# A fused four-layer block on one core: the first group's scores in halves of the ring's rows, ScalarE normalising the second batch, the Hadamard products moved behind the group

## What is computed

```python
# x: (4, 512, 256) fp32; HIDDEN 256, 16 heads of 16
def attn_a(x, Wq, bq, Wk, bk, Wv, bv, Wo, bo):
    Q, K, V = (split_heads(x @ W.T + b) for W, b in ((Wq, bq), (Wk, bk), (Wv, bv)))   # (B, 16, 512, 16)
    attn = softmax(Q @ K^T / sqrt(16), axis=-1)
    return merge_heads(attn @ V) @ Wo.T + bo
def ffn(x, W1, W2, W3):                      # H = 1024
    hidden = silu(x @ W1.T) * (x @ W3.T)
    return fwht(hidden) @ W2.T               # Walsh-Hadamard transform, normalised
def attn_b(x, Wv, Wg, bg, Wq, bq, Wo):
    store = (x @ Wv) * sigmoid(x @ Wg + bg) * sqrt(0.05)
    mem = scan(store, decay=0.95, axis=1)
    return (mem * sigmoid(x @ Wq + bq) * sqrt(0.05)) @ Wo
x = x + attn_a(layernorm(x)); x = x + ffn(layernorm(x))
x = x + attn_b(layernorm(x)); x = x + ffn(layernorm(x))
```

## Time and profile before

| what | us |
|---|---|
| median of 3 runs (586.34 to 586.47) | 586.35 |
| the profiled execution's own time | 586.26 |
| its span, first to last instruction | 584.4 |
| PE busy | 565.8 (97%) |
| DVE busy | 376.8 (64%) |
| ACT busy | 298.5 (51%) |
| POOL busy | 176.6 (30%) |

### The profile page before, as it was taken

How to read it: one execution, slowest core, us unless ns; L and a number is a source line. 1 busy time by engine, 2 the same in 40 slices (tenths; PEclk the granted TensorE clock), 3 DMA queues, 4 the chain that set the end, 5 groups by cost and what they waited for, 6 DMA issues and landing times.

```text
span 584.4 us, 8867 instructions
## 1 busy us (share of the span) xinstructions
PE 565.8 (97%) x3288; PEld 390.1 (67%) x3288; DVE 376.8 (64%) x718; ACT 298.5 (51%) x546; POOL 176.6 (30%) x193
## 2 busy tenths in 40 slices
PE   9899999999999988999999999999999999999997
PEld 4534334344334433368888888898777888888886
DVE  5498898898888899644363444558887436344433
ACT  3238878876886787752334242244445233424221
POOL 3956446354455242820101010014333010101000
PEclk9999999999999999999999999999999999999999
DMA  7654740240033030010000000000000010010101
GB/s 231 135 112 163 199 122 18 76 127 20 2 111 109 3 146 3 3 72 2 1 0 1 1 0 1 2 2 0 1 0 2 1 36 1 1 36 2 38 0 37
DMA packets 17891, 26.54 MB, mean 45 GB/s; under 512 B 2552, under 2 KB 10744, under 8 KB 17464
## 3 DMA queue, kind: packets, MB, share of 16 engines
q1 hardware_dynamic: 15992, 24.13, 13.6%
q10 hardware_dynamic: 1856, 1.84, 1.4%
HBM read 10.88 MB, written 5.24 MB: 28 GB/s over the span
## 4 chain that ended last, share of the span: by engine, by line
PE 85%; DVE 5%; ACT 4%; issue 2%; DMA 1%; POOL 1%; SPq 1%; DVEq 0%; ACTq 0%
PE PS L281 82%; PE PS L292 2%; DVE mxr L861 2%; ACT PR L735 1%; DMA ring<-ql 1%; DVE PR L1020 1%; ACT xf L644 1%; ACT qf L658 1%; DVE XNs L842 1%; ACT PR L788 1%; POOL xTl L1051 1%; ACT xTh L644 1%; PE PS L472 1%; DVE AOl L853 1%; SPq L214 1%
## 5 line engine op out<-in xcount | busy, mean ns | idle before, releaser
L281 PE MATMUL PS<-xTh,ring 128*128 128x512 f32 x608 | 188.5, 392 | 0.0
L861 DVE TENSOR_REDUCE mxr<-PS 128x1 f32<-128x512 f32 x256 | 163.0, 682 | 29.0 <-PE PS L281 28.7
L735 ACT ACTIVATE PR<-PS 128x512 f32<-128x512 f32 x256 | 137.8, 603 | 39.7 <-PE PS L281 39.7
L281 PEld LDWEIGHTS PS<-xTh,ring 128*128 128x128 f32 x608 | 113.2, 188 | 22.9 <-issue 0.8
L281 PE MATMUL PS<-xTl,ring 128*128 128x512 f32 x304 | 110.3, 391 | 0.4 <-POOL xTl L1051 0.4
L281 PE MATMUL PS<-ring 50*128 50x512 f32 (+1 forms) x512 | 98.2, 450 | 5.4 <-DVE mxr L861 4.9
L975 DVE TENSOR_TENSOR PR<-PR,PS 128x512 f32<-128x512 f32 x64 | 43.8, 684 | 91.6 <-PE PS L281 73.7
L281 PEld LDWEIGHTS PS<-ring 50*128 50x128 f32 (+1 forms) x512 | 41.2, 184 | 84.2 <-ACT PR L735 57.2
L644 ACT ACTIVATE AOh<-PR 128x512 fp32r<-128x512 f32 x72 | 45.5, 632 | 101.1 <-DVE PR L975 89.2
L1051 POOL TENSOR_TENSOR xTl<-xf,xTh 128x512 fp32r<-128x512 f32 x30 | 43.2, 1456 | 140.9 <-ACT xTh L644 140.9
L853 DVE TENSOR_TENSOR AOl<-PR,AOh 128x512 fp32r<-128x512 f32 x72 | 51.1, 710 | 50.3 <-ACT AOh L644 50.3
(11 more groups left out here) (98 smaller groups left out, 621.5 us busy)
## 6 DMA issues: line engine op xcount, KB each, us to landing
ring<-qh SPq DMA_DIRECT2D x52, 128.0 KB, 3.1
ring<-ql SPq DMA_DIRECT2D x26, 128.0 KB, 3.1
ring<-weight_scratch SPq DMA_DIRECT2D x3, 1024.0 KB, 4.9
weight_scratch<-in_w SPq DMA_DIRECT2D x2, 1024.0 KB, 6.8
out<-X SPq DMA_DIRECT2D x8, 256.0 KB, 2.2
X<-in_x SPq DMA_DIRECT2D x3, 512.0 KB, 5.2
PR<-in_w SPq DMA_DIRECT2D x1, 1024.0 KB, 7.6
ring<-AOh SPq DMA_DIRECT2D x8, 128.0 KB, 4.0
```

The costliest lines, as they stand in the source:

```text
L281: return nc.tensor.matmul(dst, lhsT, rhs, start=start, stop=stop, skip_group_check=True)
L735: nc.scalar.activation(PR[:, j % 8, :], PS[:, kq_bank(j), :], ACT.Exp, scale=HD ** -0.5)\
L861: nc.vector.tensor_reduce(mxr[:, S % 2, blk, TT * p + t:TT * p + t + 1], PS[:, QK0 + i % 3, :], AX.X, ALU.max, negate=True).then_inc(max_d ...
```

## The change

It does six things.

1. The twelve row copies for n = 0 and 1 are all issued by SP, first the six of row block 1, then the six of row block 0, each half with its own semaphore (`first_rows[blk]`). ACT issues none, and SP no longer waits for the first twelve before it issues those for n = 2 and 3.
2. The first sixteen score tiles are taken as eight of row block 1, then eight of row block 0 (`first_score`); from tile 16 on in pairs as before.
3. `keep_busy` ahead of the transposes goes from 7 to 4, the one ahead of the projections from 512 to 384 columns, and of the five between values and scores one is left. In units 9, 10 and 12 no fill is left.
4. The Hadamard products stand behind units 8, 9, 10 and 12. ACT's copies of them come after `mT`, and the split of batch 1's first transposed tile comes before the fourth one's.
5. ACT normalises batch 1 in two steps per tile (subtract the mean, multiply by the deviation's reciprocal), from a negated mean that POOL writes (`nmean`). POOL's own normalising (L1054) goes, and POOL splits the group's maxima ahead of `place_values`.
6. The eight DMAs of `wo` are issued by SP behind `max_rows(0)`; `WOh` is written by ACT in step K = 3 and `WOl` by POOL in step K = 5.

```diff
-HAD_AT = (4, 5, 6, 8)
+HAD_AT = (8, 9, 10, 12)
...
+        nmean = sb("nmean", [P, TT])
...
+        first_rows = [sem(f"first_rows{blk}") for blk in range(2)]
...
+        def first_score(i):
+
+            return (i % 8, i // 8) if i < 16 else (i // 2, i % 2)
...
-            ring_load(0, 0)
-
-            for n in range(2):
-                sp.wait_ge(ring_in[n], QDMAS)
+
+            for blk in (1, 0):
+                for n in range(2):
+                    copies = ring_rows(0, n, 0)[2 * blk:2 * blk + 2]
+                    sp.wait_ge(qk_hi, n + 1)
+                    for args in copies:
+                        sp.dma_start(*args).then_inc(first_rows[blk], DMA)
+                    copies = ring_rows(0, n, 1)[blk:blk + 1]
+                    sp.wait_ge(qk_lo, n + 1)
+                    for args in copies:
+                        sp.dma_start(*args).then_inc(first_rows[blk], DMA)
             ring_load(0, 2)
             ring_load(0, 3)
             max_rows(0)
+
+            for e in range(2):
+                for j in range(GH):
+                    r = 32 * j + HD * e
+                    sp.dma_start(OT[r:r + HD, :, :].rearrange("p a c -> p (a c)").rearrange("p (g n) -> p g n", n=D),
+                                 wo.rearrange("(g e) (j c) n -> e j c g n", e=2, c=32)[e, j, 0:HD, :, :])\
+                        .then_inc(wo_in, DMA)
...
-            def score_qk(U, h):
+            def score_qk(U, h, n=None):
                 b, p, t = U // STEPS, U % STEPS // TT, U % TT
-                i, blk = 2 * U + h, 1 - h
+                i, blk = 2 * U + h if n is None else n, 1 - h
...
-                    pe.wait_ge(ring_in[2 * mt], QDMAS * (b + 1))
-                    pe.wait_ge(ring_in[2 * mt + 1], QDMAS * (b + 1))
+
+                    pe.wait_ge(ring_in[2 * mt], QDMAS * (b + mt))
+                    pe.wait_ge(ring_in[2 * mt + 1], QDMAS * (b + mt))
...
+                if 2 * K + h < 3:
+
+                    pe.wait_ge(w2h_done, 2 * K + h + 1)
...
+                if a == 0:
+                    pe.wait_ge(w2h_done, FT // 2)
...
-            keep_busy(7, MB, SEQ)
+            keep_busy(4, MB, SEQ)
...
-            keep_busy(1, MB, SEQ)
+            keep_busy(1, MB, FILL)
...
-            keep_busy(2, PS[:, 5, :], SEQ)
-            pe.wait_ge(ring_in[0], QDMAS)
-            keep_busy(3, PS[:, 5, :], SEQ)
+            keep_busy(1, PS[:, 5, :], SEQ)
             pe.wait_ge(qk_hi, 4)
             pe.wait_ge(qk_lo, 4)
-            for U in range(LEAD):
-                for h in range(2):
-                    wait_qk(U, h)
-                    score_qk(U, h)
-                if U == 4:
-
-                    pe.wait_ge(fly_done, 3)
-                    pe.wait_ge(v_copied, 2)
-                if U in HAD_AT:
-                    j = HAD_AT.index(U)
-                    mm(PS[:, HAD_BANK[j], :], had[:, :], PR[:, 4 + j, :], True, True).then_inc(had_ready, 1)
-                elif U < 8:
+            for i in range(2 * LEAD):
+                U, h = first_score(i)
+                if i in (0, 8):
+                    pe.wait_ge(first_rows[1 - h], QDMAS)
+                if i >= 3:
+                    pe.wait_ge(max_done, i - 2)
+                score_qk(U, h, i)
+                if i % 2 and U < 8:
                     keep_busy(1, MB, FILL)
-                elif U == LEAD - 2:
-                    pe.wait_ge(xns_ready, 1)
-                    pe.wait_ge(mt_ready, 1)
-                    ln_transpose(0, MB)
-                else:
-                    pe.wait_ge(w2h_done, 3)
-                    keep_busy(1, PS[:, 2, :], FILL)
-                if U == 8:
-                    pe.wait_ge(ml_done, 1)
-                    nc.tensor.transpose(MB[0:32, 0:P], ms[:, :, :, :].rearrange("p a b k -> p (a b k)"), ident[:, :])\
-                        .then_inc(mps_ready, 1)
-            pe.wait_ge(w2h_done, FT // 2)
+                elif i % 2:
+
+                    if U == 8:
+                        pe.wait_ge(fly_done, 3)
+                        pe.wait_ge(v_copied, 2)
+                    if U in HAD_AT:
+                        j = HAD_AT.index(U)
+                        mm(PS[:, HAD_BANK[j], :], had[:, :], PR[:, 4 + j, :], True, True).then_inc(had_ready, 1)
+                    if U == 8:
+                        pe.wait_ge(ml_done, 1)
+                        nc.tensor.transpose(MB[0:32, 0:P], ms[:, :, :, :].rearrange("p a b k -> p (a b k)"), ident[:, :])\
+                            .then_inc(mps_ready, 1)
+                    if U == LEAD - 2:
+                        pe.wait_ge(xns_ready, 1)
+                        pe.wait_ge(mt_ready, 1)
+                        ln_transpose(0, MB)
...
-                act.wait_ge(ring_in[(n + 2) % 4], QDMAS * (b + (n > 1)))
+                act.wait_ge(ring_in[(n + 2) % 4], QDMAS * b)
...
-                if n == 1:
-                    for part, ready in ((0, qk_hi), (1, qk_lo)):
-                        act.wait_ge(ready, 2)
-                        for args in ring_rows(0, 1, part):
-                            act.dma_start(*args).then_inc(ring_in[1], DMA)
             for half in range(2):
                 v_evacuate(0, half, PS[:, V_BANK[half], :])
-            for n in range(2):
-                act.wait_ge(ring_in[n], QDMAS)
-
-            for e in range(2):
-                for j in range(GH):
-                    r = 32 * j + HD * e
-                    act.dma_start(OT[r:r + HD, :, :].rearrange("p a c -> p (a c)").rearrange("p (g n) -> p g n", n=D),
-                                  wo.rearrange("(g e) (j c) n -> e j c g n", e=2, c=32)[e, j, 0:HD, :, :])\
-                        .then_inc(wo_in, DMA)
+
+            act.wait_ge(nmean_done, 1)
+            act.wait_ge(rstd_done, 2)
+            act.wait_ge(lnT_ready, 2)
+            for t in range(TT):
+                nc.scalar.activation(XNs[:, t, :], X[:, TT + t, :], ACT.Identity, bias=nmean[:, t:t + 1])\
+                    .then_inc(centred, 1)
+            for t in range(TT):
+                c = slice(TT + t, TT + t + 1)
+                act.wait_ge(centred, t + 1)
+                last = nc.scalar.activation(XNs[:, t, :], XNs[:, t, :], ACT.Copy, scale=rstd[:, c])
+            last.then_inc(xns_ready, 1)
             for j in range(FT // 2):
+                if j == 0:
+                    max_evacuate(0)
                 if j == FT // 2 - 1:
-                    max_evacuate(0)
+                    ln_evacuate(1, 0, MB)
+                    ln_hi(1, 0, 0)
                 act.wait_ge(had_ready, j + 1)
                 hi(hadamard_part(j), PS[:, HAD_BANK[j], :], 1.0 / HID ** 0.5)
                 hi(W2h[:, 2 * j:2 * j + 2, :].rearrange("p f n -> p (f n)"), PS[:, HAD_BANK[j], :], 1.0 / HID ** 0.5)\
                     .then_inc(w2h_done, 1)
-            act.wait_ge(wo_in, 8 * DMA)
-            hi(WOh[:, :, :].rearrange("p g n -> p (g n)"), OT[:, :, :].rearrange("p a c -> p (a c)")).then_inc(whi_done, 1)
-            ln_evacuate(1, 0, MB)
...
+                if K == 3:
+                    act.wait_ge(wo_in, 8 * DMA)
+                    hi(WOh[:, :, :].rearrange("p g n -> p (g n)"), OT[:, :, :].rearrange("p a c -> p (a c)"))\
+                        .then_inc(whi_done, 1)
...
-            for U in range(LEAD):
-                for h in range(2):
-                    row_max(U, h)
+            for i in range(2 * LEAD):
+                row_max(*first_score(i), i)
...
+                    pool.wait_ge(mom_done, 2)
+                    nc.gpsimd.tensor_scalar(nmean[:, :], mom[:, TT:2 * TT, 0], -1.0, None, ALU.mult).then_inc(nmean_done, 1)
...
+            split_max(0)
             for g in range(GROUPS):
                 place_values(0, g)
-
-            pool.wait_ge(rstd_done, 2)
-            pool.wait_ge(lnT_ready, 2)
-            for t in range(TT):
-                last = normalise_tile(TT + t, TT + t, t)
-            last.then_inc(xns_ready, 1)
-            split_max(0)
-            pool.wait_ge(whi_done, 4)
-            lo(WOl[:, :, :].rearrange("p g n -> p (g n)"), OT[:, :, :].rearrange("p a c -> p (a c)"),
-               WOh[:, :, :].rearrange("p g n -> p (g n)")).then_inc(wol_done, 1)
...
+                if K == 5:
+                    pool.wait_ge(whi_done, 4)
+                    lo(WOl[:, :, :].rearrange("p g n -> p (g n)"), OT[:, :, :].rearrange("p a c -> p (a c)"),
+                       WOh[:, :, :].rearrange("p g n -> p (g n)")).then_inc(wol_done, 1)
```

8 lines of the change are left out of this document (4 added, 4 removed).

## The result

The changed kernel takes 594.85 us in the median of four executions (593.57 to 598.37); the kernel before, run four times beside it, 586.35 (585.37 to 586.47). The ratio is 1.0158, 95% interval 1.0114 to 1.0203: slower by 1.6%, where 579.6 was forecast. The profiled execution took 594.78.

A forecast was written before the change was run, and what follows sets the result against it. The prediction took PE to be 85% of the chain, with gains only where PE is not the limit. From 586.26, -7.3 to the first score tile and +0.55 to the first exponential gave 579.5, stated as 579.6; range 578.6 to 582.3.

The forecast's parts named there:

- Row copies, the landing: Ahead of the scores: the sixth row copy, issued by SP at 16.1, lands 3.8 us later, at 19.9.
- The rival of the late landing: Ahead of the scores: the sixth copy takes 6.2 us to land although SP is alone, total 582.0; chance 0.08.
- a landing grows with what is queued ahead and not behind: Row copies: argument that the second six do not delay the first; otherwise 583.4 instead of 579.6.
- T0: Start of the first score tile's matmul: forecast 19.95 against 27.25 before, a gain of 7.3 us.
- DVE's 0.64 still sets the pace: Score stage: tiles taken by row block load as many columns, so DVE's maxima stay 0.64 us apart.
- the rival "falls once": PE gaps near 7.5, 9.8 and 19.8: one 5.15 us slow stretch costs 2.6, total 582.2; chance 0.05.
- the rival "slower": Less fill in units 9 to 12 lowers PE's clock, which stays low in the loop over K; 589.6; chance 0.03.
- The shift of the start: Ahead of the transposes: fewer fills move all projections 2.05 us earlier, bounds 1.7 and 2.3.
- The cost of the moved Hadamard products: Maxima to exponentials: ACT's four Hadamard pairs put the first exponential 0.55 us later behind T0, bounds -0.1 and +1.5.
- Tile 8 did not wait for its rows: Score stage: the twelfth copy, needed at 25.1, causes no wait; the worst landing costs 1.0 us.
- ACT's normalising: Ahead of the scores' end: eight half-size ACT instructions, 23.2 to 28.0, cost nothing; without cover up to 4.8 us.
- The rule on partition halves that the prediction weighed: Row copies: halves serialize, read as none landing before the whole; the rival had total 583.4, chance 0.03.

The follow-up runs named there:

- a_pairs_fill9: The changed kernel with its first sixteen tiles in pairs of both row blocks, waiting for all twelve copies, and nine fills ahead instead of one; 587.01 us.
- a_ones_late: The changed kernel with the four ones-rows DMAs issued behind all the row copies instead of ahead of them; 581.74 us.
- a_fill4: The changed kernel with four fills instead of one ahead of the first score tile; median 584.43 us, ratio 0.9970 to the kernel before.
- a_ones_fill2_s256: a_ones_late with two fills ahead of the first tile and 256 columns in the fills between pairs; median 580.10 us, ratio 0.9898 to the kernel before.
- a_gate: The changed kernel with SP waiting until the first six row copies have landed before it issues the other six; 593.88 us.
- a_pairs: The changed kernel with its first sixteen tiles in pairs of both row blocks, as before, so waiting for all twelve copies; 589.50 us.
- b_nofill: The kernel before with one fill instead of five between values and scores; 585.98 us.
- b_start4_early: The kernel before with the changed kernel's shorter fills at the start, and its five later fills all ahead of the wait for rows; median 587.59 us, ratio 1.0013.
- a_s512: The changed kernel with 512 instead of 384 columns in the first group's eight fills between pairs; 599.49 us.
- a_fill5_s256: The changed kernel with five fills ahead of the first tile and 256 columns in the fills between pairs; median 583.14 us, ratio 0.9949 to the kernel before.

## Why the prediction was wrong

**What failed, in the order of the steps.**

- *Row copies, the landing.* The step took 3.8, the landing of two copies "behind four of its own, in a quiet stretch"; it measured 6.1. The rival of the late landing had the right size (6.2) for a wrong reason, the input loads. Shown: the four ones-rows DMAs, moved away, give 4.0. They were in the trace ahead of the copies, and the step gave them no effect on the landing. The argument that a landing grows with what is queued ahead and not behind missed too: with the ones-rows in place it was 4.9 with the next six copies held back, 6.1 with them following. T0 was 22.90 instead of 19.95; of the 2.95, 22.90 - 20.49 = 2.41 went with these DMAs (2.1 in the landing, 0.35 in SP's issue, which took 1.34 for the first two copies instead of 1.82). The other 0.54 is 0.24 of issue (16.34 against 16.1), 0.2 of landing and 0.1 until PE starts.
- *"Both halves' matmuls load as many columns, so DVE's 0.64 still sets the pace."* The columns are the same, but two neighbours of different row blocks take 0.43 until the next load (a_pairs_fill9) and two of one row block 0.62 to 0.66 (a_ones_late, a_fill4). With the fill of 384 columns a pair takes 1.50, and DVE waits 0.21 for each. From T0 to the first exponential this costs 20.37 - 18.70 = 1.67 (a_ones_late against a_ones_fill2_s256). The Trainium skill, page "TensorE: Matmul & The Clock Gate", section "Why this matters for your kernels", says that matmuls of few rows in distinct row groups run concurrently; the 0.43 against 0.66 agrees, and the rule spoke against this order.
- *The clock.* This is the step that decided. The forecast took a clock that stays up; the rival "falls once" priced a fall at 2.6, half of the start's slow 5.15 us; the rival "slower" had the mechanism, PE at its lower level in the score stage, but put it behind the ninth unit and saw its cost in the loop over K. Measured: it fell ahead of the first tile, held 23.9 us, and cost 31.12 - 20.37 = 10.75, through DVE's waits (eight pairs at 1.44 against 0.21 are 9.8 of it), while the loop over K ran at 1.00 in full length. The argument against, "the idle 1.65 us was followed by passes at 0.43", held for that profile alone: a_gate fell behind 1.66, and of the executions of the kernel before that were run beside the experiments one took 590.2 at 0.994, some 7 us at the lower level by the estimate.

The terms are 2.41 + 0.54 + 1.67 + 10.75 + 0.1 (18.70 against 18.6) = 15.47, which is 54.02 - 38.55. They must close, for each is a difference of two rows of the table; what they tell is which run separates which part, one profiled execution each.

**Gap or order?** The gap is shown to matter; the part of the order is not settled. For the gap: with it filled or shortened, the clock was at 0.999 or 1.0 in eight of eleven executions of a_fill4, in the one of a_ones_late and in four of four of a_ones_fill2_s256, while the changed kernel's four were all at 0.974 to 0.980. For the order: in the old order, profiles with gaps of 3.90 and 6.09 were back 4.1 and 6.8 us after T0, and the stretch to the first exponential grew by 1.5 and by 3.05 (a_pairs against a_pairs_fill9), where the new order's four profiles stayed low for 20.5 to 30.7 us. The expectation for b_nofill went by the gap alone, and missed by 11. Against the order as a rule: b_start4_early, in the old order, had an execution that was low for some 20 us and took 9.6 more than the fastest of its kernel, near the 10.75 that the changed kernel lost, and three executions in the new order were low for only some 3.5 us. Over all executions of the study at a mean clock of 0.997 or less, the estimate gives 20 us or more for eight of eleven in the new order and for one of fourteen in the old (two of them of the kernel before). So long stays went with the new order, in kernels that differ in fills and gaps too; neither order ensures its kind.

**What was right.** The shift of the start: forecast 2.05, measured 2.03 (`xTh`) to 2.09 (first transpose). The cost of the moved Hadamard products: forecast 0.55, measured 0.53 (a_pairs_fill9) and 0.64 (18.70, the kernels with 256 columns). Tile 8 did not wait for its rows (a_ones_late: DVE's waits are 0.21 throughout). ACT's normalising lay under the wait for the maxima, as costed at nothing. `WOh` starts at 58.98 without a wait. From the first exponential on the length is the same within 0.2. The kernel that comes nearest to the forecast, a_ones_fill2_s256, has a median of 580.1 where 579.6 was forecast; it moves the ones-rows, which the forecast did not know of, and its T0 of 21.28 is set by its two fills.

**What stays open.** Why equal gaps have unequal outcomes: 1.65 kept the clock (before), 1.66 lost it (a_gate), and of eleven executions of a_fill4 eight kept it, two lost it shortly and one, behind a gap of 0.94, for 20.5 us; b_start4_early's went from no loss to 20 us. The rows show that it happens, not what tips it, nor what ends a stay. Whether the pairs or the products of unit 8 have a part in that was not tried alone.

## What to carry to other kernels

Before a copy on the critical path, look at what the same queue was given just ahead of it, and at how many DMA engines each of those transfers uses: small DMAs of two partitions that nobody waits for yet can hold a large one that everybody waits for (6.1 us to landing here instead of 4.0), and an earlier start upstream then only makes a longer gap. When an order of small matmuls is changed, price the pairs by their row blocks as well as by their columns (0.43 against 0.66 here). And a gap that has done no harm in one profile is no proof that the next kernel can bear it, nor even the next execution of the same one: read the granted clock over the windows behind the gap, and the mean clock of several executions.

## What the runs showed of the hardware that was not expected

- **DMAs of two partitions can hold up a large copy behind them.** With the second half held back (a_gate), the DMA share fell to 0.16 of 16 engines, 34 GB/s, from 19 us on while the sixth copy was outstanding; with the four two-partition DMAs moved, the copy landed after 4.0 instead of 6.1. The Trainium skill, page "DMA: Bandwidth & Descriptors", section "Why a DMA increments its semaphore by 16 and not by 1", says that a DMA is spread over the largest number of engines, up to 16, that divides the slowest dimension of both its sides, and that they are the lowest-numbered ones; for two partitions that is two. The 0.16 is 2.6 engines' worth over those 2 us, which agrees roughly; which engines they were, the rows do not say. The rule on partition halves that the prediction weighed does not hold for the first half's landing: it came 4.0 after issue with six more copies behind it.
- **The lower clock can last though PE is busy.** In four profiles whose neighbouring small matmuls were of one row block it held for 20.5 to 30.7 us, with PE busy all the time by the profile from the first tile on (after, a_gate, a_fill4's, a_s512); in profiles with neighbours of different row blocks, 3.4 us in all (b_nofill) or until 6.8 behind T0 (a_pairs). Other executions, by their mean clocks, went against this both ways.
- **Executions of one kernel spread with the clock.** b_start4_early took 583.2 in one and 592.8 in another, at mean clocks of 1.0 and 0.983, with the other eight between; a_fill4 and a_fill5_s256 had one execution each at 0.983.
